# Own products in fp32 instead of split fp16, and 16 of 25 transposed blocks copied by VectorE, in a two-layer graph kernel

## The chip, the cores and the metric

The kernel runs on one core of a Trainium2 chip. The metric is the device time of one execution in microseconds (us). Engines are named as in the profile: PE is TensorE's matmul row and PEld its weight loads, DVE is VectorE, ACT is ScalarE, POOL is GpSimd, SP is the engine that issues the DMAs.

## The reference

There are 3125 nodes with 256 features and 50000 edges (`src`, `dst`, sorted by `dst`). What is computed, cut to its core:

```
# block 0: twice, with (W0, b0), (W1, b1)
deg   = number of edges of each row;  vals = 1 / max(deg, 1)[rows]
neigh = segment_sum(vals * x[cols], rows)
x     = relu(concat(x, neigh) @ W.T + b)
x     = layernorm(x_in + x)
# block 1
h_self = x @ W_self;  h_sparse = keep the 32 largest of each row of (x @ W_neigh)
x      = layernorm(x + h_self + segment_sum(h_sparse[src], dst) / max(deg_dst, 1))
```

## The kernel before

The kernel turns the list of edges into a dense matrix of counts, C, of 3125 x 3125 in fp16, and every sum over neighbours into matmuls with blocks of C. Nodes are cut into 25 blocks of 125.

**Head.** The edges are loaded and turned into a table of slots of up to 128 edges. Matmuls with one-hot `pick` matrices (line 1363, twice: a first set of 125 columns, a second of 500; 100 rows deep) fetch the slots. PE's clock is kept up by matmuls on a tile of ones, 128 rows deep (`keep_clock`, line 1327). The weights W0 and W1 are transposed on PE (`weights_t`) and copied out (`weights_out`, line 1030) to `w_t[0]` and `w_t[1]`. The semaphore `matched` then selects the fast branch (`quick_copies`, `fills`); a slow branch for other lists of edges is not run here.

**Build.** For t = 0 to 24 one slab of C, 125 rows by 3125 columns, is made in four sets of windows (7, 6, 6 and 6). For each set, DVE writes one-hot matrices (`quick_hots`, line 639), PE multiplies them (`fill`, line 1380) into one of two PSUM pairs, and ACT copies the result out (`quick_copy`, line 1078). SP stores the slab to DRAM (line 351). One step later the slab is also transposed, block by block, on PE (`transposes`, line 1459) in four groups g; groups 0 and 2 are copied to `ct` by ACT (`tr_copy`, line 1116), groups 1 and 3 by DVE (line 782). `TG` gives the blocks in each group: 5, 8, 5, 7. DVE writes the one-hots of step t+1 during step t. Each engine works in the order in which `fills`, `quick_copies` and DVE's loop have the calls; the rest is done by semaphores.

**Own products.** For each block t of x the kernel needs x @ [W0 self half | W0 neighbour half]. PE transposes the block into PSUM bank 7 (`own_transposes`, line 1479, fp32). ACT scales it and writes it in fp16 (`own_t`, line 1121), and DVE writes the fp16 rest (`own_low`, line 775). PE then does six fp16 matmuls of 512 columns with the split weights `w0_parts` (`own_product`, line 1467, three for each half h). ACT copies the result from bank 6 to `own` (`own_copy`, line 1128). SP stores one half of `own` (line 355); POOL splits the other into two fp16 parts for the first aggregation (`split_a0`, lines 520 and 522). The table `OWN` says in which step each product stands: none before step 4, one in most steps, two in steps 7, 9, 11 and 13.

**Scales.** The fp16 splits need a scale for each tensor. ACT sums squares of x, of the two weights of block 1 and of the bias (`square_x`, `square_weights`), takes roots (`roots`), PE transposes the statistics and broadcasts the scales (`bounds_t`, `bounds_row`, `scales_b`), and DVE computes them (`bound_rows`, `bounds`, `scales_out`; lines 727 to 764) in steps 2 and 3. The weights are split by `w_high` (ACT, line 1138) and `w_low` (DVE, line 770), six of each. The split weights of the later products are stored to DRAM after slab 6 (line 364); ACT waits for them at the start of step 8 (`w_stored`), since the tiles are then written over.

**After the build** come two aggregations of 1250 matmuls in all (line 1567) with products between them, and the last sum with 625 (line 1679). The change does not touch them.

Of the kernel before, what the change touches and what calls it, by code (L numbers as in the profile page):

```python
# [70 lines left out]
TG = [5, 8, 5, 7]  # L71
TG0 = [0, 5, 13, 18]
# [9 lines left out]
def gnn(nc, x, src, dst, w0, b0, w1, b1, wself, wneigh, out):  # L82
    ctx = ExitStack()
    with ctx:
# [52 lines left out]
        w0_parts = bld("w0_parts", [128, 2, 2, 2 * F], F16)  # L137
        x_t16 = bld("x_t16", [128, 4, 128], F16)
        w_junk = x_t16[:, :, :].rearrange("p k n -> p (k n)")
# [10 lines left out]
        w_t = [held[l]("w_t%d" % l, [128, 4, F], F32) for l in range(2)]  # L150
# [7 lines left out]
        squares = held[5]("squares", [128, 10], F32)  # L158
        norms = held[5]("norms", [128, 10], F32)
# [117 lines left out]
        squared, rooted = sem("squared"), sem("rooted")  # L277
# [9 lines left out]
        own_tlo, own_staged, a0_hi, a0_split = sem("own_tlo"), sem("own_staged"), sem("a0_hi"), sem("a0_split")  # L287
# [21 lines left out]
        def halves(i):  # L309

            if i < 4:
                l, h = divmod(i, 2)
                out = (w0_parts, w_parts[0])[l][:, h].rearrange("p q (a f) -> p q a f", a=2)
                return out[:, 0], out[:, 1], w_t[l][:, h::2, :], scales[:, 3 + l:4 + l]
            at = (i - 4) * F
            out = w_parts[1][:, :, :, at:at + F]
            return out[:, :, 0, :], out[:, :, 1, :], (ws_nat, wn_nat)[i - 4][:, :, :], scales[:, 1 + i:2 + i]
# [9 lines left out]
        def _(sp):  # L327
# [134 lines left out]
        def _(pool):  # L462
# [20 lines left out]
            nc.gpsimd.memset(squares[:, :], 0.0).then_inc(const_ready, 1)  # L483
# [80 lines left out]
        NCONST = 24  # L564
# [3 lines left out]
        def _(dve):  # L568
# [155 lines left out]

            def bound_rows():
# [4 lines left out]
            def bounds():  # L730
# [9 lines left out]

                step(v.tensor_tensor(bound[:, :], sv[:, 0, 0::2], sv[:, 0, 1::2], ALU.max))
# [4 lines left out]
                step(v.tensor_scalar(bound[:, 2:3], sparse_sum[:, :], 1.43 * F ** 0.5, None, ALU.mult))  # L746
# [81 lines left out]
            with dve.If(total > E - 1):  # L828
                for t in range(1, NT):
                    more, own = t + 1 < NT, OWN[t]  # L830
                    if more:
                        quick_hots(t + 1, 0)
                    if t == 3:
# [9 lines left out]
                    if 2 < t < 6:  # L843
                        w_low(2 * t - 5)
                    if t == 3:
                        own_low(0)
# [4 lines left out]
                    if t == 2:  # L851
                        bounds()
# [3 lines left out]
                    if len(own) > 1:  # L856
                        own_low(own[1] + 1)
# [4 lines left out]
            with dve.If(total < E):  # L862
                general_table()
                clear_tr()
                bound_rows()
# [4 lines left out]
                for i in range(6):  # L870
                    w_low(i)
                with dve.Fori(1, NT) as t:
                    for u in range(WT):
# [3 lines left out]
                        if u == 2:  # L877
                            own_low(t - 1)
                own_low(NT - 1)
# [125 lines left out]
        def _(act):  # L1005
# [41 lines left out]
            def square_x(c):  # L1047
                act.wait_ge(x_loaded[c], BOTH)
                if c:
# [3 lines left out]
                             accum_out=squares[0:P, c:c + 1]).then_inc(squared, 1)  # L1053

            def square_weights():
                act.wait_ge(eye_added, 2)
                act.wait_ge(wn_loaded, 16)
                act.wait_ge(b_loaded, 16)
                for k, (m, n) in enumerate(((ws_nat[:, :, :].rearrange("p c f -> p (c f)"), 2 * F),
                                            (wn_nat[:, :, :].rearrange("p c f -> p (c f)"), 2 * F), (bcol[:, :], 2))):  # L1060
                    act.wait_ge(squared, 4 + k)
                    a.activation(w_junk[:, 0:n], m, ACT.Square, scale=TINY, accum_out=squares[:, 4 + 2 * k:5 + 2 * k]).then_inc(squared, 1)

            def roots():
                act.wait_ge(squared, 7)
                a.activation(norms[:, :], squares[:, :], ACT.Sqrt).then_inc(rooted, 1)
                act.wait_ge(rooted, 1)
                a.activation(stat[:, 0:4], norms[:, 0:4], ACT.Copy, scale=1.0 / TINY).then_inc(stat_ready, 1)
# [663 lines left out]
```

## Time and profile before

| what | value |
|---|---|
| three timed runs | 697.01, 697.11, 700.86 us; median 697.11 us |
| the profiled execution | 701.42 us, span 699.6 us |
| busy in the span | PE 641.8 (92%), DVE 505.9 (72%), ACT 348.7 (50%), POOL 106.9 (15%) |
| build loop, steps 1 to 24 | from 36 to 194 us of the span |
| DMA | 73.08 MB, mean 104 GB/s |

Times in a row are us from the start of the span. Starts are recorded more sharply than ends: neighbours on one engine overlap in the records, so what an instruction takes of its engine is read from its start to the next start. PEclk is the granted clock of TensorE as a share of 2.4 GHz.

### The profile page before, as it was taken

To read this page: it belongs to the slowest core of one execution; us is meant where nothing else is said; L and a number is where in the kernel's file an instruction comes from. 1 tells how busy PE (TensorE), PEld (TensorE's weight loads), DVE (VectorE), ACT (ScalarE), POOL (GpSimd) and SP (SyncE) were. 2 spreads that over 40 slices of the span, in tenths; PEclk is the share of its full clock that TensorE was granted. 3 is DMA by queue.
4 is the path that set the end of the run, shared out by engine and by line. 5 is a ranking of instruction groups with operands and counts; after the bars stand their busy time and mean duration, and the time that the engine had idled before them with its cause. 6 is when DMAs were issued, how large, how long until landed. Compare 5 with 4: busy or idle time off the path is not lost.

```text
span 699.6 us, 11372 instructions
## 1 busy us (share of the span) xinstructions
PE 641.8 (92%) x4012; PEld 338.4 (48%) x4013; DVE 505.9 (72%) x1296; ACT 348.7 (50%) x669; POOL 106.9 (15%) x188
## 2 busy tenths in 40 slices
PE   8867788888787999999999999999999889999996
PEld 3355566666643444444444444444444334444443
DVE  8659989999768788888883578787877844634433
ACT  3588888899847777777774223333333220100000
POOL 3001222222111001010100222323232210000000
PEclk9789999999998999999999999999999999999999
DMA  9423554555531011111111555555656414310000
GB/s 212 91 91 113 188 162 137 162 161 158 157 101 37 29 43 33 41 34 40 36 40 39 156 174 164 172 167 169 176 162 182 121 36 135 115 47 23 22 28 25
DMA packets 39542, 73.08 MB, mean 104 GB/s; under 512 B 3120, under 2 KB 32207, under 8 KB 39481
## 3 DMA queue, kind: packets, MB, share of 16 engines
q1 hardware_dynamic: 39481, 72.30, 34.8%
q8 instruction: 34, 0.56, 0.4%
q14 instruction: 27, 0.22, 0.1%
HBM read 38.91 MB, written 33.38 MB: 103 GB/s over the span
## 4 chain that ended last, share of the span: by engine, by line
PE 72%; DVE 17%; ACT 7%; issue 2%; DMA 2%; POOL 0%; SPq 0%; ACTq 0%; DVEq 0%; POOLq 0%
PE pair L1567 36%; PE bank L1679 9%; PE pair L1679 8%; PE bank L1467 7%; DVE hots L639 6%; PE pair L1467 4%; PE bank L1459 2%; DVE ct L782 2%; ACT own L1128 2%; DVE x_t L775 2%; PE bank L1473 1%; PE pair L1363 1%; DMA own_in<-own_dram 1%; ACT x_t L1121 1%; ACT slab L1078 1%
## 5 line engine op out<-in xcount | busy, mean ns | idle before, releaser
L1567 PE MATMUL pair<-xs,ct 125*128 125x512 f16 x625 | 144.1, 381 | 0.0
L1567 PE MATMUL pair<-a,ct 125*128 125x512 f16 x625 | 142.8, 379 | 0.0
L639 DVE TENSOR_TENSOR hots<-iota,jobs 125x1792 f16<-125x1792 f16 (+1 forms) x100 | 104.5, 1063 | 1.3 <-PE pair L1380 0.7
L1567 PEld LDWEIGHTS pair<-xs,ct 125*128 125x128 f16 x625 | 61.3, 100 | 68.7 <-issue 1.8
L1567 PEld LDWEIGHTS pair<-a,ct 125*128 125x128 f16 x625 | 61.0, 99 | 68.1
L1078 ACT ACTIVATE slab<-pair 125x875 f16<-125x875 f32 (+1 forms) x100 | 83.4, 858 | 5.6 <-PE pair L1380 4.1
L1245 ACT ACTIVATE a<-ct 125x1000 f16<-125x1000 f16 (+1 forms) x75 | 80.2, 1069 | 0.9
L1679 PE MATMUL bank<-xs,ct 125*128 125x512 f16 (+1 forms) x325 | 71.5, 379 | 0.0
L1679 PE MATMUL pair<-xs,ct 125*128 125x512 f16 x300 | 66.4, 379 | 0.0
L1459 PE MATMUL bank<-ident,slab 125*128 125x125 f16 x625 | 52.7, 224 | 14.0 <-DVE ct L782 9.9
L1318 ACT ACTIVATE sd<-mv,epsb 125x1 f32<-125x1 f32 x25 | 7.4, 294 | 113.9 <-DVE mv L998 113.9
L531 POOL TENSOR_TENSOR own_in<-own_in,bias_sb 125x256 f32<-125x256 f32 x50 | 37.2, 744 | 173.8 <-DMA own_in<-own_dram 173.7
L1380 PE MATMUL pair<-hots 125*128 125x125 f16 x625 | 52.8, 224 | 11.5 <-ACT slab L1078 8.4
L895 DVE SCALAR_TENSOR_TENSOR t<-pair,rdeg,own_in 125x256 f32<-125x256 f32 x50 | 24.2, 484 | 54.2 <-PE pair L1567 48.3
L1459 PEld LDWEIGHTS bank<-ident,slab 125*128 125x128 f16 x625 | 40.2, 101 | 27.1 <-issue 14.4
L1221 ACT ACTIVATE tr_sb<-bank 128x500 f16<-128x500 f32 x50 | 29.0, 580 | 45.1 <-PE bank L1473 45.1
L1679 PEld LDWEIGHTS bank<-xs,ct 125*128 125x128 f16 (+1 forms) x325 | 32.3, 100 | 37.8
L1380 PEld LDWEIGHTS pair<-hots 125*128 125x128 f16 x625 | 41.1, 100 | 17.0 <-issue 11.7
L1467 PE MATMUL bank<-w_parts,x_t 128*125 128x512 f16 x150 | 41.2, 383 | 7.5 <-DVE x_t L775 7.5
L1679 PEld LDWEIGHTS pair<-xs,ct 125*128 125x128 f16 x300 | 29.8, 99 | 34.4
L782 DVE COPY ct<-bank 125x1008 f16<-125x1008 f16 (+1 forms) x50 | 32.0, 641 | 15.3 <-PE bank L1459 15.3
L1467 PE MATMUL pair<-w_lay,tr_sb 128*128 128x512 f16 x150 | 36.9, 382 | 3.8 <-ACT tr_sb L1221 3.8
(213 smaller groups left out, 852.9 us busy)
## 6 DMA issues: line engine op xcount, KB each, us to landing
c_dram<-slab SPq DMA_DIRECT2D x25, 683.6 KB
ct<-c_dram SPq DMA_DIRECT2D x25, 683.6 KB
own_in<-own_dram SPq DMA_DIRECT2D x50, 125.0 KB
own_dram<-own SPq DMA_DIRECT2D x25, 125.0 KB
own_dram<-own_st SPq DMA_DIRECT2D x25, 125.0 KB
x_in<-in_x_dram SPq DMA_DIRECT2D x25, 125.0 KB
z_dram<-z_st SPq DMA_DIRECT2D x25, 125.0 KB
a<-z_dram SPq DMA_DIRECT2D x5, 625.0 KB
```

Of the source, the lines that this page charges most:

```text
L531: nc.gpsimd.tensor_tensor(own_in[k % 2][:, :], own_in[k % 2][:, :], bias_sb[:, :], ALU.add).then_inc(own_biased, 1)
L639: v.tensor_tensor(hots[k][:, :, :, :].rearrange("p w g (a d) -> p (w g) a d", d=2), iota, job, ALU.is_equal).then_inc(win_hot, 1)
L782: v.tensor_copy(ct[:, TG0[g]:TG0[g] + TG[g], t, :], tr16[1][0:P, 0:TG[g], 0:PC]).then_inc(tr_free[1], 1)
L895: return noted(v.scalar_tensor_tensor(t2[k % 2][:, :], agg[k % 3][0:P, 0:F], rdeg[l][:, T:T + 1], own_in[k % 2][:, :], ALU.mult, ALU.add))
L1078: a.activation(slab3[t % 2][:, :, lo * QW:hi * QW].rearrange("p b (w d) -> p b w d", d=QW), pair[f % 2][0:P, 0:n, 0:QKEY].rearrange("p w ( ...
L1221: a.activation(tr_sb[i % 2][:, :, 0:P], tp[i % 2], ACT.Copy).then_inc(tp_copied, 1)
L1245: a.activation(unread[:, 0:(hi - lo) * P].rearrange("p (b s) -> p b s", s=P), ct[:, lo:hi, T, 0:P], ACT.Copy, accum_out=deg_part[:, T, k:k ...
L1380: last = mm(pair[f % 2][:, u, 0:QKEY], hots[f][:, u, 0, :], hots[f][:, u, 1, 1:QKEY + 1], start=True, stop=True, skip_group_check=True)
L1459: last = nc.tensor.transpose(tr16[g % 2][:, i, 0:P], slab[par][:, (TG0[g] + i) * P:(TG0[g] + i) * P + 128], ident16[:, 0:P])
L1467: last = mm(out, lhs(2 * pt + h), w[:, h, q, :], start=h == 0 and k == 0, stop=h == 1 and k == 2, skip_group_check=True)
L1567: ins = mm(agg[k % 3][0:lhs.shape[1], :], lhs, parts[l][:, t, :], start=t == 0, stop=t == NT - 1, skip_group_check=True)
L1679: ins = mm(out3[T % 8][0:lhs.shape[1], :], lhs, xs[:, b, :], start=b == 0, stop=b == NT - 1, skip_group_check=True)
```

## The change

Four things are changed.

1. The own products are done in fp32. `own_t` writes the transposed block unscaled in fp32, `own_low` is gone, each half of a product is one fp32 matmul call with 512 columns, and the W0 split (two of six `w_high` and `w_low`) is gone. `own_copy` uses another scale. The tile of W0 moves out of the place that is reused later.
2. `TG` becomes 4, 8, 5, 8: ACT copies 9 blocks in a step where it copied 10, DVE 16 where it copied 15.
3. Products start at step 3 and two stand in steps 8, 13 and 18 alone. The scales come earlier: `bounds_t`, `bounds_row` and `scales_b` are all in step 2. The statistics of the last part of x, of the weights of block 1 and of the bias are now largest absolute values found by DVE in step 1, where ACT had summed squares; the square root is done by DVE as one more small instruction on the bits.
4. In the head, one `keep_clock` matmul of 512 columns follows each group of three pick matmuls of the second set (eight in all), behind a wait for `wt_copied`. The `keep_clock` matmuls of step 2 are gone.

```diff
-OWN = {0: [], 1: [], 2: [], 3: [], 4: [0], 5: [1], 6: [2], 7: [3, 4], 8: [5], 9: [6, 7], 10: [8], 11: [9, 10], 12: [11],
-       13: [12, 13], **{t: [t] for t in range(14, NT)}}
+TWOS = (8, 13, 18)
+OWN = {t: [] for t in range(3)}
+for _t in range(3, NT):
+    _n = sum(map(len, OWN.values()))
+    OWN[_t] = [_n, _n + 1] if _t in TWOS else [_n]
-KEEP = {0: 4, 1: 2, 2: 1}
+KEEP = {0: 4, 1: 2}
-TG = [5, 8, 5, 7]
+TG = [4, 8, 5, 8]
...
+            def largest_x(c):
+                dve.wait_ge(x_loaded[c], BOTH)
+                v.tensor_reduce(stat[0:P, c:c + 1], xs32[:, XC[c]:XC[c + 1], :].rearrange("p t f -> p (t f)"), X, ALU.max,
+                                apply_absolute_value=True).then_inc(stat_ready, 1)
...
-            def own_low(t):
-
-                dve.wait_ge(own_tcopied, t + 1)
-                v.scalar_tensor_tensor(x_t16[:, 2:4, 0:P], xp, scales[:, 0:1], x_t16[:, 0:2, 0:P], ALU.mult, ALU.subtract
-                                       ).then_inc(own_tlo, 1)
...  (DVE's loop)
+                    if t == 1:
+                        largest_x(3)
+                    if t == 2:
                         dve.wait_ge(cols_copied, 4)
-                        scales_out()
+                        bound_rows()
                     tr_copy(t - 1, 1)
-                    if 2 < t < 6:
+                    if 2 < t < 5:
                         w_low(2 * t - 6)
...
+                    if t == 1:
+                        largest_w()
                     if t == 2:
-                        bound_rows()
+                        bounds()
...
-                    if own and own[0] + 1 < NT:
-                        own_low(own[0] + 1)
...
+                    if t == 2:
+                        scales_out()
...  (ACT)
-                a.activation(x_t16[:, 0:2, 0:P], xp, ACT.Copy, scale=scales[:, 0:1]).then_inc(own_tcopied, 1)
+                a.activation(x_t32[:, :, :], xp, ACT.Copy).then_inc(own_tcopied, 1)
...
-                    if t == 1:
-                        square_x(3)
-                    if t == 1:
-                        square_weights()
-                    if t == 1:
-                        roots()
...  (PE)
+                        if k:
+                            keep_clock(bank[7], 1)
                 last.then_inc(picked, 1)
+                if k == 0:
+                    pe.wait_ge(wt_copied, 2)
...
-                    pe.wait_ge(own_tlo, t + 1)
+                    pe.wait_ge(own_tcopied, t + 1)
                     pe.wait_ge(own_copied, t + 1)
-                    pe.wait_ge(w_split, 2)
-                last = in_parts(bank[6][0:P, :], lambda k: x_t16[:, k, 0:P], w0_parts, (h,))
+                    pe.wait_ge(wt_copied, 2)
+                last = mm(bank[6][0:P, :].rearrange("p (a f) -> p a f", a=2), x_t32[:, h, :], w0_t[:, h::2, :], start=h == 0, stop=h == 1,
+                          skip_group_check=True)
...  (SP)
-                    sp.wait_ge(w_split, 6)
+                    sp.wait_ge(w_split, 4)
```

In PE's loop, the second half of a product now stands ahead of the transposes of group 1, where it stood behind them.

## Rows read from the trace of the kernel before

**Rows 1.** The page, part 4: the chain that ended last, shares by engine.

```profile
PE 72%; DVE 17%; ACT 7%; issue 2%; DMA 2%; POOL 0%; SPq 0%; ACTq 0%; DVEq 0%; POOLq 0%
```

**Rows 2.** Busy time by stretch: length, PE, PEld, DVE, ACT, POOL, clock, DMA.

```profile
157.00:168.00 11.00, 9.20 (x114) 7.09 (x112) 10.88 (x15) 9.89 (x16) 2.39 (x4) 1.00 0.52 165
...
16.00:26.00 10.00, 10.00 (x24) 3.21 (x25) 6.59 (x15) 2.89 (x5) 0.00 (x0) 0.51 0.98 190
```

**Rows 3.** Timeline of one late step, DVE, then POOL: start, us, instruction.

```profile
171.08 0.67 DVE L782 COPY ct<-bank 125x1008 f16<-125x1008 f16 x1
171.67 0.94 DVE L639 TENSOR_TENSOR hots<-iota,jobs 125x1536 f16<-125x1536 f16 x1
172.67 0.48 DVE L775 SCALAR_TENSOR_TENSOR x_t<-bank,scales,x_t 128x250 f16<-128x250 f32 x1
173.07 2.23 DVE L639 TENSOR_TENSOR hots<-iota,jobs 125x1536 f16<-125x1536 f16 x2
175.22 0.60 DVE L782 COPY ct<-bank 125x882 f16<-125x882 f16 x1
175.75 1.07 DVE L639 TENSOR_TENSOR hots<-iota,jobs 125x1792 f16<-125x1792 f16 x1
...
172.95 0.67 POOL L522 TENSOR_TENSOR xs<-own,xs 125x256 f16<-125x256 f32 x1
```

**Rows 4.** Timeline of ACT: the same place in two late steps.

```profile
171.59 0.69 ACT L1128 ACTIVATE own<-bank,unscale 125x512 f32<-125x512 f32 x1 [0.56 <-PE bank L1467]
...
177.26 0.69 ACT L1128 ACTIVATE own<-bank,unscale 125x512 f32<-125x512 f32 x1 [0.55 <-PE bank L1467]
```

**Rows 5.** Timeline of PE in that step.

```profile
171.39 0.38 PE L1479 MATMUL bank<-identx,xs 125*128 125x125 f32 x2
171.61 0.50 PE L1380 MATMUL pair<-hots 125*128 125x125 f16 x6
...
176.41 0.81 PE L1467 MATMUL bank<-w_parts,x_t 128*125 128x512 f16 x3
177.06 0.38 PE L1479 MATMUL bank<-identx,xs 125*128 125x125 f32 x2
```

**Rows 6.** Timeline of DVE: first one-hots issued in steps 5, 9, 11 and 23.

```profile
70.45 1.08 DVE L639 TENSOR_TENSOR hots<-iota,jobs 125x1792 f16<-125x1792 f16 x1
...
96.09 1.08 DVE L639 TENSOR_TENSOR hots<-iota,jobs 125x1792 f16<-125x1792 f16 x1
...
109.41 1.08 DVE L639 TENSOR_TENSOR hots<-iota,jobs 125x1792 f16<-125x1792 f16 x1
...
181.42 1.08 DVE L639 TENSOR_TENSOR hots<-iota,jobs 125x1792 f16<-125x1792 f16 x1
```

**Rows 7.** Instructions of line 1394, two fp32 matmul calls: count, min/median/max ns.

```profile
L1394 PE MATMUL bank<-onesq,hits x4: 163/163/164, 32.7 to 32.8; 125*1 125x1 f32 x4
```

**Rows 8.** Timeline of DVE in steps 1 to 3; last, line 651's group.

```profile
36.66 1.09 DVE L639 TENSOR_TENSOR hots<-iota,jobs 125x1792 f16<-125x1792 f16 x1 [0.32 <-PE pair L1380]
...
49.71 0.68 DVE L782 COPY ct<-bank 125x1008 f16<-125x1008 f16 x1 [4.21 <-PE bank L1459]
...
52.44 0.17 DVE L739 COPY sv<-bank 1x32 f32<-1x32 f32 x1
...
54.74 0.16 DVE L752 TENSOR_SCALAR srow<-svi 1x8 f32<-1x8 f32 x1
...
58.94 0.75 DVE L770 SCALAR_TENSOR_TENSOR w_parts<-w_t,scales,w_parts 128x512 f16<-128x512 f32 x1 [0.43 <-ACT w_parts L1138]
...
L651 DVE TENSOR_REDUCE stat<-w_nat 128x1 f32<-128x512 f32 x4 | 2.5, 674 | 0.0
```

**Rows 9.** Timeline of ACT and SP around the store of the split weights.

```profile
80.81 1.64 ACT L1078 ACTIVATE slab<-pair 125x750 f16<-125x750 f32 x2
...
82.46 1.89 SPq L364 DMA_DIRECT2D wparts_dram<-w_parts  x2
...
89.24 0.93 ACT L1078 ACTIVATE slab<-pair 125x875 f16<-125x875 f32 x1 [0.35 <-DMA wparts_dram<-w_parts]
```

More of the change, by code:

```diff
@@ L149, in gnn @@
         held = [Arena(ct_at + (b * REG + HELD * PC) * 2, ct_at + (b + 1) * REG * 2) for b in range(19, NT)]
-        w_t = [held[l]("w_t%d" % l, [128, 4, F], F32) for l in range(2)]
+        w_t = [w0_t, held[1]("w_t1", [128, 4, F], F32)]
         ws_nat = held[2]("ws_nat", [128, 2, F], F32)
@@ L745, in bounds @@
                 step(v.tensor_tensor(sparse_sum[:, :], sv[:, 1, 12:13], sv[:, 1, 13:14], ALU.add))
-                step(v.tensor_scalar(bound[:, 2:3], sparse_sum[:, :], 1.43 * F ** 0.5, None, ALU.mult))
+                step(v.tensor_scalar(bound[:, 2:3], sparse_sum[:, :], 1.01 * F ** 0.5, None, ALU.mult))
                 step(v.tensor_scalar(bound[:, 5:6], bound[:, 5:6], 1.0, None, ALU.add))
@@ L864, in _ @@
                 clear_tr()
+                largest_x(3)
+                largest_w()
                 bound_rows()
@@ L869, in _ @@
                     general_hots(u)
-                for i in range(6):
+                for i in range(4):
                     w_low(i)
@@ L1052, in square_x @@
                 a.activation(x_junk[:, 0:n], xs32[:, XC[c]:XC[c + 1], :].rearrange("p t f -> p (t f)"), ACT.Square, scale=TINY,
[L1053 to L1068, printed above, removed]
-                a.activation(stat[:, 10:16], norms[:, 4:10], ACT.Copy, scale=1.0 / TINY).then_inc(stat_ready, 1)
+                             accum_out=stat[0:P, c:c + 1]).then_inc(squared, 1)
             def quick_copy(t, f):
@@ L1127, in own_copy @@
                 act.wait_ge(a0_split, t + 1)
-                a.activation(own[:, par, :], bank[6][0:P, :], ACT.Copy, scale=unscale[0:P, 4:5]).then_inc(own_copied, 1)
+                a.activation(own[:, par, :], bank[6][0:P, :], ACT.Copy, scale=scales[0:P, 1:2]).then_inc(own_copied, 1)
             def ready_for_own():
@@ L1170, in quick_copies @@
                         own_copy(own[1], own[1] % 2, own[1] // 2)
-                        own_t(own[1] + 1)
-                    if 2 < t < 5:
-                        w_high(2 * t - 4)
-                        w_high(2 * t - 3)
+                        if own[1] + 1 < NT:
+                            own_t(own[1] + 1)
                 for g in (0, 2):
@@ L1181, in copies @@
                 ready_for_own()
-                for i in range(6):
+                for i in range(4):
                     w_high(i)
@@ L1206, in _ @@
                 square_x(2)
-                square_x(3)
-                square_weights()
-                roots()
                 act.wait_ge(win_read, FILLS - 1)
@@ L1416, in bounds_t @@
             def bounds_t():
-                pe.wait_ge(stat_ready, 2)
+                pe.wait_ge(squared, 3)
+                pe.wait_ge(stat_ready, 4)
                 pe.wait_ge(w_sums, 4)
@@ L1526, in fills @@
                     transposes(t - 1, par, 0)
+                    fill(t, 1)
                     if t == 2:
-                        bounds_t()
-                    fill(t, 1)
+                        bounds_row()
                     if t in KEEP:
                         keep_clock(bank[7], KEEP[t])
-                    transposes(t - 1, par, 1)
                     if own:
                         own_product(own[0], 1)
-                    if t == 3:
+                    transposes(t - 1, par, 1)
+                    if t == 2:
                         own_transposes(0, xs32[:, 0, :])
@@ L1543, in fills @@
                     if t == 2:
-                        bounds_row()
+                        scales_b()
                     if len(own) > 1:
@@ L1551, in fills @@
                         own_product(own[1], 1)
-                        own_transposes(own[1] + 1, xs32[:, own[1] + 1, :])
+                        if own[1] + 1 < NT:
+                            own_transposes(own[1] + 1, xs32[:, own[1] + 1, :])
                     transposes(t - 1, par, 3)
```

69 lines of the change are left out of this document (34 added, 35 removed).

## The prediction

> **What bounds the kernel now.** I read the page's chain first: PE holds 72% of it and DVE 17% [rows 1]. The aggregations and the last sum are PE alone, and the change leaves them as they are; DVE's share lies in the build. So only the stretch up to 194 us can move, and what follows it moves along by the same amount. The busy times by stretch come next. In a late stretch of 11 us DVE is busy 10.88, PE 9.20, ACT 9.89, at full clock (1.00, which is 2.4 GHz), with the DMA engines at 0.52 [rows 2]. DVE is full, the DMA is not. The timeline of one step says the same without the overlap of records: ACT's `own` copies stand 5.67 us apart and ACT has an idle gap of 0.55 before each [rows 4], while DVE goes from one instruction to the next without a gap: 0.59 for the 8-block copy, 1.00 for a set of one-hots (its last 0.1 is a wait for ACT's `own_t`, whose end `own_low` needs), 0.40 for `own_low`, 2.15 for two sets, 0.53 for the 7-block copy, 1.00 for the wide set. That is 5.67 [rows 3]. A step with one product is bound by DVE.
>
> In the steps before 14, singles and doubles alternate. From step 9 to step 11, three products, DVE's first one-hots move on by 13.32 [rows 6], 1.98 more than two singles. There the chain product, `own_copy`, `own_t`, `own_low`, next product is the bound, and the same kind of group takes every step pair from 7 to 13.
>
> **The change, part by part.** The sum is made on the profiled execution, 701.42 us, which lies 4.3 above the median of 697.11; I carry the difference over to the median, since nothing in the build's steady rows depends on which run it is.
>
> *DVE in a single step.* Removed: `own_low`, 0.40, and the wait of 0.13 before it (1.00 against 0.87 for a set that has no wait, the rate of the second set of the pair). Added: one block on the last copy, 0.59 for 0.53, so 0.06. 5.67 - 0.53 + 0.06 = 5.20; I use 5.21. In it is a stall: the pair of sets takes 2.15 where twice 0.87 would be 1.74, and POOL's subtraction runs from 172.95 while the first of them starts at 173.07 [rows 3]. After the change `own_copy` starts about when PE comes to group 1's transposes, so POOL's cast and subtraction end up beside the set behind the 8-block copy, again with the subtraction a little ahead of it. I keep 0.41.
>
> *PE in a single step.* Three fp16 matmuls of 512 columns take 0.65 from their first start, 176.41, to that of the next instruction, 177.06, so one is 0.216 [rows 5]. The rows of before show no fp32 matmul of that width. Two rows bound it. A call in fp32 leaves two records: line 1394 has two calls and four records [rows 7]. A record in fp32 with 125 columns (line 1479) takes 0.11, from 171.39 to 171.61 for two, and one in fp16 with as many 0.055, from 171.61 for six [rows 5]. Lower bound: two records at the fp16 rate, 0.43 for a half. Nearest row: two records at twice the rate, 4 x 0.216 = 0.86. Upper bound: the 0.11 is a fixed cost in part and hides a steeper rate, 4 times per record, 1.72. I take 0.86, since the fp32 row is the one of the same kind. PE then has 50 fills and transposes at 0.055 (2.75), two halves (1.72) and the fp32 transposes (0.22): 4.7, below DVE's 5.21.
>
> *ACT in a single step.* 5.67 - 0.55 = 5.12 occupied, less one block of about 0.1: 5.0. The fp32 output of `own_t` is taken at the price of the fp16 one. ACT too is below 5.21, but by 0.2 alone. Laid out in order (fill 0.34 to 0.39, half 0.86, group 0, fill, half, group 1, own transposes, fill, group 2, fill, group 3), PE reaches group 1 about 0.5 before DVE has freed its bank, so DVE stays the bound. Behind the product's second half, which moved ahead of group 1's transposes, waits DVE's copy of that group; those 0.5 cover it, and without them a single would be 5.7.
>
> *Double steps.* From group 1: own transposes, fill, group 2, 1.3; the second product waits for `own_t`, until 1.5; its halves, the fill between and the own transposes, 2.3; group 3, 0.4; then the next step's first fill and the wait for ACT's second `own_t`, until 4.9; half, group 0, fill, half, 2.3. Sum 7.2, and the step behind it gains 0.1: 7.1. ACT waits in it, not DVE.
>
> *Steps 5 to 22.* Before, 70.45 to 181.42, 111.0 [rows 6]. After, 15 x 5.21 + 3 x 7.1 = 99.5. **-11.5.**
>
> *Steps 1 to 4.* Before, 36.66 to 70.45, 33.8, in which DVE was idle 4.21 before one copy alone, waiting for PE and, through it, for the squares and roots of ACT [rows 6, 8]. After, DVE has 16 sets (14.4), 8 copies (4.7), `largest_x` of 1536 columns at the 0.60 that 512 take from start to start (0.674 recorded; 1.8), `largest_w` (1.3), `bound_rows` (0.4), `bounds` with 13 small instructions (2.3 for 12 from 52.44 to 54.74, so 2.5), `scales_out` (0.6), four `w_low` of 0.75 recorded, 0.65 taken (2.6) [rows 8], two stalls by POOL (0.8), and 1.5 of waits for PE's group 1 in steps 1 and 2, the second behind `bounds_row`, for which PE now stops until `bound_rows` is done. Sum 30.6 to 31.0. **-2.8.** ACT loses 5 us of squares, roots and a table load here; it is not the bound, and I count nothing more for that.
>
> *Store of the split weights.* SP issues it 1.65 after ACT's fourth copy of step 6 starts (80.81 to 82.46), and ACT is released at 89.24, 6.8 after the issue [rows 9]. Before, a double step lay between and the wait was 0.35. Now only 5.21 + 0.7 - 1.65 = 4.3 lie between the issue and the first copy of step 8, so ACT will stand for 2.5, and step 8 is a double, where ACT is on the path. **+2.0** (0 to 2.5).
>
> *Head.* Eight matmuls of 512 columns are added to 24 picks that lie on the chain. From 16 to 26 us PE is busy for all of 10.00 us, and the clock stays at 0.51, its lower level of 1.2 GHz [rows 2]. At that level the eight cost 8 x 0.43 = 3.4 and give nothing. If they bring the clock to the upper level at once, the picks take 5 where they took 10 and the eight cost 1.7, so -3.3. If the clock rises part of the way through, about -1. I take **-1**. The Trainium skill ("TensorE: Matmul & The Clock Gate", section "What's actually happening") says that the gate's ratio follows how busy PE has been. By that rule these picks would have run at full speed and the eight would be +1.7; rows 2 speak against it as stated, since PE was busy throughout and the clock stayed low. The wait for `wt_copied` costs nothing: the copies are ahead of ACT's first `slots_out`, which is done by then.
>
> *Tail and rest.* In step 23 DVE's saving and in step 24 the longer product (0.43) cancel: 0. DMA: about 0.9 MB of slab and own rows each step, 0.52 of the engines at 5.67, 0.57 at 5.21: covered.
>
> Sum: -11.5 - 2.8 + 2.0 - 1.0 = -13.3, so 688.1 for the profiled execution and **683.8** for the median.
>
> **The rivals.**
>
> *A, the stall by POOL changes.* If POOL's pair falls clear of the one-hots, DVE needs 4.8 and ACT's 5.0 is the bound, with its order 4.9 to 5.0: 18 steps x 0.25 = 4.5 less, 679. If both POOL instructions stop DVE (the cast is 0.53 recorded, 0.4 alone), 0.4 x 18 = 7 more, 691. For the second speaks that DVE now has one-hots back to back where `own_low` stood. The Trainium skill ("SBUF — State Buffer", section "Who interferes with whom") says that a DVE instruction with two inputs in SBUF and a GpSimd one that reads it exclude each other, first come first served. The stall of 0.41 in rows 3 agrees; the rule lets either order come out.
>
> *B, the head stays at the low clock.* +3.4 in place of -1: 688. For it: ten microseconds at full use did not raise the clock. Against it: the tile of ones is dense and fills the array, and the picks are one-hot and 100 rows deep.
>
> *C, PE becomes the bound, slower than before.* If a half takes more than 1.2, PE's own work passes DVE's: 4.7 + 2 x (1.2 - 0.86) = 5.4, with the order's gaps 5.7. That is the point. At the upper bound of 1.72 PE needs 6.4 in a single and about 10 in a double: 15 x 6.4 + 3 x 10 = 126 against 111, +15; with the rest 697 + 15 - 3 + 1 = 710. Only the small fp32 rows speak on it, and they speak for 0.86.
>
> *D, a product ahead of group 1 delays it.* The move of the second half costs DVE a wait in each step, singles stay at 5.6 to 5.7, and only doubles, three for four, and the early steps pay: 691 to 693. Against it: the 0.5 of room in the layout.
>
> **How the numbers follow.** Forecast as summed (679 to 688, singles at 5.0 to 5.4): 0.60. A's gain 0.08, A's loss 0.08, B 0.13 (which still is 688), D 0.06, C 0.05. A measurement of this kernel can tell about 1%, 7 us, from no change. Faster by more than that, under 690.1: the forecast, A's gain, B and a part of A's loss: 0.87. Within 1%: the rest of A's loss and D: 0.09. Slower: 0.04. The range leaves out C and half of D and of A's loss above, and little below: 677 to 691.
>
> **What would show it.** Right: own products of 0.86 a half, no line 775, singles of 5.2 with DVE without gaps, doubles of about 7.1, an ACT gap of 2 to 3 by the store of the split weights at step 8, and a clock above 0.51 in the stretch of the second picks. Wrong: halves over 1.2, gaps of DVE before the copy of group 1 in every step, or second picks that take longer than before.

## The result and the profile after

| | median us | runs | ratio to before (95%) |
|---|---|---|---|
| before | 697.14 | 697.01, 697.11, 697.18, 700.86 | |
| after | 689.93 | 688.79, 689.49, 690.37, 690.46 | 0.9892 [0.9864, 0.9921] |
| after, on a second chip | 691.04 | six, 689.56 to 694.91 | 0.9894 [0.9855, 0.9932] |

The kernel became 7.2 us faster, 1.1%. The forecast was 683.8, 13.3 faster, with a range of 677 to 691: the sign and the range held, the size was about half. The steady steps did what was forecast; steps 1 to 4, where 2.8 were to be won, lost time.

The page of the kernel after: span, busy times, the granted clock in 40 slices, the chain that ended last.

```profile
span 688.5 us, 11240 instructions
...
PE 649.0 (94%) x3966; PEld 335.5 (49%) x3967; DVE 498.1 (72%) x1274; ACT 338.6 (49%) x654; POOL 106.4 (15%) x187
...
PEclk9967999999999999999999999999999899999999
...
PE 84%; DVE 8%; ACT 3%; DMA 2%; issue 2%; SPq 0%; POOL 0%; DVEq 0%; ACTq 0%; POOLq 0%
```

DVE's share of the chain fell from 17% [rows 1] to 8% and PE's rose from 72% to 84%. The third and fourth slices of the clock (34 to 69 us) have 6 and 7: that is the early part of the build.

**A steady step.** DVE in one step (start, us, instruction):

```profile
136.47 0.67 DVE L791 COPY ct<-bank 125x1008 f16<-125x1008 f16 x1
137.07 3.04 DVE L637 TENSOR_TENSOR hots<-iota,jobs 125x1536 f16<-125x1536 f16 x3
140.03 0.67 DVE L791 COPY ct<-bank 125x1008 f16<-125x1008 f16 x1
140.63 1.07 DVE L637 TENSOR_TENSOR hots<-iota,jobs 125x1792 f16<-125x1792 f16 x1
141.62 0.67 DVE L791 COPY ct<-bank 125x1008 f16<-125x1008 f16 x1
```

Against [rows 3], `own_low` is gone, both copies have eight blocks, and there is no gap. The step takes 141.62 - 136.47 = 5.15, where it took 5.67. The three sets take 2.96; three at 0.87 would be 2.61, so 0.35 is a stall. It lies beside POOL's subtraction:

```profile
136.89 0.67 POOL L520 TENSOR_TENSOR xs<-own,xs 125x256 f16<-125x256 f32 x1
```

PE in the step:

```profile
137.31 0.60 PE L1445 MATMUL bank<-ident,slab 125*128 125x125 f16 x8
...
138.24 1.08 PE L1479 MATMUL bank<-w_t,x_t 128*125 128x512 f32 x2
139.16 0.39 PE L1445 MATMUL bank<-ident,slab 125*128 125x125 f16 x4
139.38 0.50 PE L1365 MATMUL pair<-hots 125*128 125x125 f16 x6
139.71 1.08 PE L1479 MATMUL bank<-w_t,x_t 128*125 128x512 f32 x2
```

One half of a product is two records and holds PE for 0.92, from 138.24 to 139.16. Three fp16 matmuls of the same width took 0.65 [rows 5].

**Stretches by engine** (window, length, PE, PEld, DVE, ACT, POOL, clock, DMA share, GB/s): the head, the early steps, and a late stretch as in [rows 2].

```profile
16.00:26.00 10.00, 10.00 (x58) 4.70 (x56) 7.95 (x17) 5.24 (x8) 0.00 (x0) 1.00 1.06 189
46.00:59.00 13.00, 9.11 (x50) 6.23 (x50) 6.98 (x25) 4.83 (x7) 0.40 (x1) 0.50 0.19 61
...
137.00:148.00 11.00, 10.82 (x117) 7.57 (x115) 11.00 (x14) 10.63 (x18) 2.70 (x5) 1.00 0.54 170
```

In the late stretch DVE is full and ACT and PE are close to it. In the second row nothing is full: DVE works 6.98 of 13.00, PE 9.11, and the clock stands at 0.50, 1.2 GHz.

**Step 3.** DVE in it, then PE (in brackets the idle time before an instruction, and its releaser):

```profile
52.61 0.15 DVE L780 TENSOR_TENSOR unscale<-unscale,scales 128x1 f32<-128x1 f32 x1
52.68 1.08 DVE L637 TENSOR_TENSOR hots<-iota,jobs 125x1792 f16<-125x1792 f16 x1
58.68 0.68 DVE L791 COPY ct<-bank 125x1008 f16<-125x1008 f16 x1 [4.92 <-PE bank L1445]
...
65.01 1.08 DVE L637 TENSOR_TENSOR hots<-iota,jobs 125x1792 f16<-125x1792 f16 x1
```

```profile
52.91 2.04 PE L1479 MATMUL bank<-w_t,x_t 128*125 128x512 f32 x2 [0.78 <-issue]
54.74 0.62 PE L1445 MATMUL bank<-ident,slab 125*128 125x125 f16 x4
...
55.79 2.02 PE L1479 MATMUL bank<-w_t,x_t 128*125 128x512 f32 x2
57.60 1.04 PE L1445 MATMUL bank<-ident,slab 125*128 125x125 f16 x8
```

DVE finishes the scales (`scales_out`, last row at 52.61), and 0.3 later PE starts the first product, after an idle time of 0.78. The fp32 product does not read the scales. But it waits for `own_copied`, which ACT first raises in `ready_for_own`, once DVE has written the last scale (`unscale_ready`); and it writes bank 6, where the scales stand until DVE has copied them, at 52.05. The halves take 1.83 and 1.81, and the eight transposes of group 1, for which DVE waits, start at 57.60. So DVE stands for 4.92, and step 3 takes 65.01 - 52.68 = 12.33, where step 3 of the kernel before took 7.57 and 7.56 in two profiled executions.

**The store of the split weights.** SP issues it, and ACT waits for it at the start of step 8. SP, then ACT:

```profile
81.50 1.90 SPq L363 DMA_DIRECT2D wparts_dram<-w_parts  x2
```

```profile
88.69 0.92 ACT L1068 ACTIVATE slab<-pair 125x875 f16<-125x875 f32 x1 [2.81 <-DMA wparts_dram<-w_parts]
```

DVE's first one-hots of steps 8, 9 and 10, which answer to [rows 6]:

```profile
87.52 1.07 DVE L637 TENSOR_TENSOR hots<-iota,jobs 125x1792 f16<-125x1792 f16 x1
95.34 1.59 DVE L637 TENSOR_TENSOR hots<-iota,jobs 125x1792 f16<-125x1792 f16 x1
102.44 1.07 DVE L637 TENSOR_TENSOR hots<-iota,jobs 125x1792 f16<-125x1792 f16 x1
```

A double step shows in these marks one step later, since DVE is ahead: 7.10 in step 9 is the double of step 8, and the 7.82 in step 8 hold ACT's wait.

**Where the time went**, by the same marks in each profiled execution: DVE's first one-hots of steps 0, 1, 5 and 23, as in [rows 6], then the first matmul of the first aggregation and the start of its last one. Before was profiled twice; the second execution (696.29 us) lies nearer to the median.

| us | before, first | before, second | after | after - first | after - second |
|---|---|---|---|---|---|
| until the one-hots of step 0 | 32.60 | 28.42 | 29.63 | -3.0 | +1.2 |
| step 0 | 4.06 | 4.44 | 4.40 | +0.3 | 0.0 |
| steps 1 to 4 | 33.79 | 32.14 | 37.98 | +4.2 | +5.8 |
| steps 5 to 22 | 110.97 | 111.0 | 101.66 | -9.3 | -9.3 |
| tail of the build | 12.0 | 12.2 | 10.6 | -1.4 | -1.6 |
| first aggregation | 183.4 | 182.1 | 180.2 | -3.2 | -1.9 |
| all behind it | 322.8 | 324.2 | 324.0 | +1.3 | -0.2 |

### The profile page after: what moved, and what is told of

Read it like the earlier page. It is cut to its first block, busy times and chain, and to the rows that moved or that the text cites. A ratio compares the mean times of both kernels' runs of the same rounds, so it can differ in the third digit from the quotient of the medians.

```text
span 688.5 us, 11240 instructions
## 1 busy us (share of the span) xinstructions
PE 649.0 (94%) x3966; PEld 335.5 (49%) x3967; DVE 498.1 (72%) x1274; ACT 338.6 (49%) x654; POOL 106.4 (15%) x187
## 4 chain that ended last, share of the span: by engine, by line
PE 84%; DVE 8%; ACT 3%; DMA 2%; issue 2%; SPq 0%; POOL 0%; DVEq 0%; ACTq 0%; POOLq 0%
PE pair L1555 36%; PE bank L1667 10%; PE pair L1667 9%; PE bank L1479 6%; PE bank L1445 5%; PE pair L1453 5%; PE bank L1453 5%; PE pair L1365 4%; DVE hots L637 2%; PE bank L1459 1%; DMA own_in<-own_dram 1%; DMA wparts_dram<-w_parts 1%; PE pair L1344 1%; PE bank L1465 1%; ACT a L1226 1%
## 5 line engine op out<-in xcount | busy, mean ns | idle before, releaser
L1068 ACT ACTIVATE slab<-pair 125x875 f16<-125x875 f32 (+1 forms) x100 | 83.2, 856 | 11.4 <-PE pair L1365 7.0
L1479 PE MATMUL bank<-w_t,x_t 128*125 128x512 f32 x100 | 56.0, 642 | 1.8 <-ACT x_t L1111 1.0
L1365 PEld LDWEIGHTS pair<-hots 125*128 125x128 f16 x625 | 41.4, 101 | 10.2 <-issue 7.8
L791 DVE COPY ct<-bank 125x1008 f16<-125x1008 f16 x50 | 33.7, 673 | 14.5 <-PE bank L1445 14.5
```

Of the source, the lines that this page charges most:

```text
L791: v.tensor_copy(ct[:, TG0[g]:TG0[g] + TG[g], t, :], tr16[1][0:P, 0:TG[g], 0:PC]).then_inc(tr_free[1], 1)
L1068: a.activation(slab3[t % 2][:, :, lo * QW:hi * QW].rearrange("p b (w d) -> p b w d", d=QW), pair[f % 2][0:P, 0:n, 0:QKEY].rearrange("p w ( ...
L1365: last = mm(pair[f % 2][:, u, 0:QKEY], hots[f][:, u, 0, :], hots[f][:, u, 1, 1:QKEY + 1], start=True, stop=True, skip_group_check=True)
L1479: last = mm(bank[6][0:P, :].rearrange("p (a f) -> p a f", a=2), x_t32[:, h, :], w0_t[:, h::2, :], start=h == 0, stop=h == 1, skip_group_ch ...
```

## The experiments

Times of runs are medians; the ratio is to the kernel before, timed in the same set of runs (its medians there: 697.39, 697.53 and 697.04).

### Head: the fillers alone, and the change without them

e3 puts the eight fillers into the kernel before; e4 is that kernel unchanged, for a second profile of it; e2 takes the fillers out of the change.

```diff
(e3, against before)
+                        if k:
+                            keep_clock(bank[7], 1)
                 last.then_inc(picked, 1)
+                if k == 0:
+                    pe.wait_ge(wt_copied, 2)
(e2, against after)
-                        if k:
-                            keep_clock(bank[7], 1)
```

> The kernel before with the eight matmuls among the second picks alone, behind the same wait. Theory 1: 694 (3 us under 697.1), picks ending near 23.6 us with the clock at 1.00. Rival (the low clock in the head of the profiled execution was peculiar to it, which was 4.3 above the median): 697 to 699, since typical executions of before ran their picks at full clock already and the eight only add 1.7.

> The kernel before, unchanged, for a second trace. The profiled execution of before was 701.4 against a median of 697.1. If the low clock during the picks (16 to 26 us, worth 3 us) is peculiar to that execution, this one ends its picks near 22 us; if it is there in every execution, they end near 26.8 again, and a time near 697 lacks something else: the two low stretches at 208 and 219 us, in the first aggregation, which cost some 3 us against the changed kernel's trace.

> The changed kernel without the eight matmuls on the tile of ones among the second picks; all else is as in the changed kernel. Theory 1: they keep the clock up through the picks (1.00 from 16 to 26 us against 0.51 before) and are worth the 3.0 us by which the head ended earlier; then this kernel takes 692.5 to 693.5 and its picks end near 26.8 us at the low clock. Rival: the clock of that stretch falls in some executions only, by the moment at which the program starts; then this kernel's picks may run at full clock as well, end 1.7 us earlier than the changed kernel's, and the time is 688 to 690.

Measured: e3 698.75, 0.9997 [0.9966, 1.0027]; e2 691.50, 0.9930 [0.9902, 0.9958], against 0.9892 and 0.9894 for the change with them. The stretch 16 to 22 us of e4 (no fillers), and then of e5 (below, with fillers), columns as above:

```profile
16.00:22.00 6.00, 6.00 (x31) 2.52 (x29) 5.28 (x15) 2.89 (x5) 0.00 (x0) 1.00 1.13 222
```

```profile
16.00:22.00 6.00, 6.00 (x17) 2.04 (x15) 5.28 (x14) 2.89 (x5) 0.00 (x0) 0.50 1.13 222
```

The second picks run at the upper level without fillers and at the lower one with them; the row of before [rows 2] had them at the lower level too. Of the four profiled executions without fillers, two had a low clock in the picks (before and e12); of the ten with them, six, e8 among them, for which the upper level was expected. At the upper level the one-hots of step 0 come at 27.8 and 28.4 without the fillers and at 29.1 to 29.6 with them; where 6.8 us are at the lower level, at 31.1 and at 32.2 to 32.7. So at an equal clock the fillers cost about 1.2 to 1.3 by the means (29.35 against 28.1, and 32.4 against 31.1), with 0.7 to 1.8 between single executions. Four executions and ten are too few to say whether fillers change how often the clock is low. In the medians 1.3 us, 0.2%, can't be told from nothing.

### Steps 1 to 4: missing fillers, or the product ahead of group 1

There were two theories on step 3. The first: the clock is low because the fillers of step 2 are gone. The second: PE's queue has the first product, which waits until the scales are written, ahead of group 1's transposes, which don't wait for that, and the low clock makes this longer. e1 gives step 2 fillers again, eight where before had four; e5 starts the products at step 4, so that none stands in step 3; e6 does both, with two fillers at each place; e8 is the change unchanged.

```diff
(e1: after each of the first two places of KEEP in fills)
+                    if t == 2:
+                        keep_clock(bank[7], 4)
(e5; in e6 also KEEP = {0: 4, 1: 2, 2: 2})
-TWOS = (8, 13, 18)
-OWN = {t: [] for t in range(3)}
-for _t in range(3, NT):
+TWOS = (8, 12, 16, 20)
+OWN = {t: [] for t in range(4)}
+for _t in range(4, NT):
...  (ACT's own_t(0) and PE's own_transposes(0))
-                    if t == 2:
+                    if t == 3:
```

> The changed kernel with four matmuls on the tile of ones behind the first and behind the second fill of step 2, eight in all (the kernel before had one behind each of the four fills). Step 3 took 12.33 us in the changed kernel's trace, where I had forecast 6.4, with the clock at 0.50 from 46 to 59 us. Theory 1: the clock fell because TensorE has little to do in step 2 and stayed low into step 3, where the fp32 halves take 0.98 per record at that clock against 0.48. Then this kernel's step 3 is 6 to 8 us, the stretch from 46 to 59 is mostly at 1.0, and the time is 684 to 686 (4 to 6 under the changed kernel's 689.9). Rival: the clock falls in that stretch whatever step 2 holds, since it is the fp32 halves and the waits of step 3 that keep it low, or the step is long through the wait for the scales; then step 3 stays at 11 to 13 us and the time at 689 to 691, plus up to 1 for the eight matmuls.

> The changed kernel with its products from step 4 on (transposes of block 0 in step 3, doubles in steps 8, 12, 16 and 20) in place of step 3 (doubles in 8, 13, 18). In the changed kernel VectorE was idle 4.92 us in step 3 ahead of its copy of group 1. Theory 2: TensorE's in-order queue held it up: the first product waits for the scales (VectorE's last work of step 2) and both its fp32 halves stand ahead of group 1. Then step 3 falls from 12.3 to about 7.5, step 4 stays near 7, and the fourth double costs 1.9: 3 us net, 686 to 688 beside 689.9. Rival (theory 1 in its weak form: the clock at its low level alone makes step 3 long): step 3 stays at 9 us or more, since the clock is low there with the product or without, and the time is 689 to 692.

> The kernel of the run before this one (products from step 4) with two matmuls on the tile of ones behind each of the four fills of step 2. Theory 1: they shorten the stretch at the low clock around step 3 and step 3 is a further 1 us shorter. Rival: as with the eight matmuls put into step 2 of the changed kernel, where step 2 grew to 12.1, the low stretch stays and they cost 0 to 2 us.

> The changed kernel, unchanged, beside the others on one chip and with more rounds: 0.989 of the kernel before again (0.986 to 0.992). In its trace, singles of 5.15 to 5.2 and doubles of 7.1 whatever the head does; step 3 between 10.5 and 12.5; the clock of the second picks at its upper level throughout or for most of it.

| | median, ratio (95%) | steps 1, 2, 3, 4 | sum | DVE idle in it |
|---|---|---|---|---|
| before, second | | 7.43, 10.48, 7.56, 6.67 | 32.1 | 6.4 |
| after | 689.93, 0.9892 [0.9864, 0.9921] | 8.64, 10.01, 12.33, 7.00 | 38.0 | 9.5 |
| e8 after again | 691.04, 0.9894 [0.9855, 0.9932] | 8.32, 10.42, 11.49, 7.00 | 37.2 | 8.7 |
| e1 | 692.90, 0.9922 [0.9897, 0.9948] | 8.55, 12.13, 10.77, 7.00 | 38.5 | 10.0 |
| e5 | 690.19, 0.9864 [0.9821, 0.9906] | 8.20, 10.43, 7.42, 7.00 | 33.1 | 4.6 |
| e6 | 690.51, 0.9896 [0.9858, 0.9934] | 8.64, 11.28, 7.73, 7.00 | 34.7 | 6.0 |

DVE in step 3 of e5; compare the copy with that at 58.68 above.

```profile
55.48 1.08 DVE L637 TENSOR_TENSOR hots<-iota,jobs 125x1792 f16<-125x1792 f16 x1
56.73 0.68 DVE L791 COPY ct<-bank 125x1008 f16<-125x1008 f16 x1 [0.17 <-PE bank L1445]
...
62.90 1.08 DVE L637 TENSOR_TENSOR hots<-iota,jobs 125x1792 f16<-125x1792 f16 x1
```

Without a product in step 3, the wait is 0.17 instead of 4.92, though the clock is at its lower level there too, until 56.4; and the step takes 7.42 instead of 10.92 to 12.33 (six profiled executions with the product there and no fillers in step 2). The second theory is shown. Fillers in step 2 are not the cure: with e1's step 2 grows by 1.7 to 2.1, and DVE still waits 3.56 before the copy in step 3; in e6 they cost 1.2 over e5 in steps 2 and 3.

The clock has a large share in it all the same. In e1 the second half of the product ran at the upper level:

```profile
57.26 2.04 PE L1479 MATMUL bank<-w_t,x_t 128*125 128x512 f32 x2 [0.78 <-issue]
...
60.12 1.08 PE L1479 MATMUL bank<-w_t,x_t 128*125 128x512 f32 x2
...
61.68 0.68 DVE L791 COPY ct<-bank 125x1008 f16<-125x1008 f16 x1 [3.56 <-PE bank L1445]
```

The wait is 1.4 shorter there than in after. e2, without any of these fillers, had most of its second half at the upper level too and waited 3.71, so this isn't the fillers' doing. With the first half (0.92 less) and what stands between the halves (0.51 less) at the upper level as well, 2.1 of wait would be left: an estimate from e1's rows, since no run had it so. By that estimate over half of the 4.92 is the low clock, and the rest the place of the product. The lower level lasts 13.6 us around step 3 in after, 10.3 in e5, 10.2 in e6 with its fillers, and 3.4 in before's second execution; why it lasts so long in the kernels of the change stays open. Nor did a run change the order alone: the second half, which the change moved ahead of group 1, is 1.81 of the 4.92; the first half stood ahead of group 1 before as well.

e5 pays for its gain with a fourth double step, 1.9, and the store of the split weights is still in it. By the median it is level with the change (690.19 for 691.04 in the same set of runs; 686 to 688 was expected), by its ratio a little ahead, with intervals that overlap.

### Steps 8 and 9: the store of the split weights

e7 moves the first double step to 7, as a double step lay there before. e9 is e5 with the store issued one slab earlier, which the earlier scales allow.

```diff
(e7)
-TWOS = (8, 13, 18)
+TWOS = (7, 13, 18)
(e9: e5, and on SP)
-                if t == HELD - 2:
+                if t == HELD - 3:
```

> The changed kernel with the first double step at 7 in place of 8. The split weights are stored after slab 6 and ScalarE waits for them at the start of step 8; with the double between, the wait has 2 us more of cover. Forecast: steps 7 to 9 take 7.1 + 5.2 + 5.2 plus a wait of 0 to 0.6, so about 2 us less than the 5.16 + 7.82 + 7.10 of the changed kernel, in the trace and in the time (688). Rival: the 2.6 us in steps 8 and 9 are the double's own and move to step 7 with it: then no change.

> The changed kernel with products from step 4 (doubles in 8, 12, 16, 20) and the split weights stored after slab 5 in place of slab 6, one step earlier than where ScalarE stands for them. This is the version that the runs so far point to. Forecast: steps 1 to 4 take 33.0 (37 to 38 in the changed kernel), steps 8 and 9 take 12.3 together (14.9 to 16.6), steps 5 to 22 101.1 with four doubles; 686.5 to 688, about 0.985 of the kernel before. Rival: the earlier store meets the slab stores and only moves the wait to the slab copies of steps 6 and 7; then steps 5 to 22 stay at 103 to 104 and the time at 690.

Measured: e7 689.16, 0.9856 [0.9820, 0.9891]; e9 **686.49** (685.48 to 688.10), 0.9841 [0.9802, 0.9881]. First one-hots of steps 7 to 10 in e7:

```profile
84.04 1.07 DVE L637 TENSOR_TENSOR hots<-iota,jobs 125x1792 f16<-125x1792 f16 x1
89.21 1.59 DVE L637 TENSOR_TENSOR hots<-iota,jobs 125x1792 f16<-125x1792 f16 x1
96.52 1.07 DVE L637 TENSOR_TENSOR hots<-iota,jobs 125x1792 f16<-125x1792 f16 x1
101.98 1.07 DVE L637 TENSOR_TENSOR hots<-iota,jobs 125x1792 f16<-125x1792 f16 x1
```

and of steps 8, 9 and 10 in e9, and the issue of its store:

```profile
81.95 1.08 DVE L637 TENSOR_TENSOR hots<-iota,jobs 125x1792 f16<-125x1792 f16 x1
87.38 1.58 DVE L637 TENSOR_TENSOR hots<-iota,jobs 125x1792 f16<-125x1792 f16 x1
94.47 1.08 DVE L637 TENSOR_TENSOR hots<-iota,jobs 125x1792 f16<-125x1792 f16 x1
```

```profile
70.78 1.88 SPq L363 DMA_DIRECT2D wparts_dram<-w_parts  x2
```

Steps 7 to 9 take 17.95 in e7 (84.04 to 101.98) and 5.16 + 7.82 + 7.10 = 20.1 in after. Steps 8 and 9 take 12.52 in e9 (81.95 to 94.47) and 14.92 in after (87.52 to 102.44), at the same number of products. So the store cost 2.1 to 2.4 against these two, and 2.6 against a single and a double of the steady kind (5.2 + 7.1). In e8, e1, e2 and e10, four of the eight profiled executions with this wait, step 8 took 9.3 to 10.3, with 3.4 us of it at the lower clock: there the wait came to 4.2 or more over a single. e9 is faster than the kernel before, clear of noise. Against the change its ratio is lower by 0.005, with intervals that overlap at their ends: likely faster, not shown.

### The steady step: POOL, the block, and own_low alone

e10 takes away POOL's read beside the one-hots (a memset in place of the subtraction, so the low part of the first aggregation's operand is left out). e11 gives the block back to ACT. e12 is the kernel before with `own_low` left out (so that part of the own products is not computed), all else as it was.

```diff
(e10)
-                nc.gpsimd.tensor_tensor(xs[:, t, F:2 * F], a0, xs[:, t, 0:F], ALU.subtract).then_inc(a0_split, 1)
+                nc.gpsimd.memset(xs[:, t, F:2 * F], 0.0).then_inc(a0_split, 1)
(e11)
-TG = [4, 8, 5, 8]
+TG = [5, 8, 5, 7]
(e12, against before: DVE, then PE)
-                dve.wait_ge(own_tcopied, t + 1)
-                v.scalar_tensor_tensor(x_t16[:, 2:4, 0:P], xp, scales[:, 0:1], x_t16[:, 0:2, 0:P], ALU.mult, ALU.subtract
-                                       ).then_inc(own_tlo, 1)
+                pass
-                    pe.wait_ge(own_tlo, t + 1)
+                    pe.wait_ge(own_tcopied, t + 1)
```

> The changed kernel in which GpSimd writes zeros where it subtracted (the low fp16 part of the own product is left out), so it reads nothing from SBUF in that instruction. In the changed kernel's single step one set of one-hots takes 1.23 from start to start beside the subtraction, and 0.87 without. If the subtraction alone causes that, VectorE needs 4.83, ScalarE's 5.0 becomes the bound, and singles are 4.9 to 5.0; 15 singles and 3 doubles give 3 to 4 us, 686 to 687. Rival: ScalarE or TensorE already set 5.19 and VectorE's stall is cover: singles stay at 5.15 to 5.2.

> The changed kernel with the transposed blocks shared as before: 5, 8, 5 and 7, so VectorE copies 15 and ScalarE 10. If VectorE is the bound of a single step, singles fall by 0.06 to 5.12, about 1 us in all, below what the timing can tell. If ScalarE is close behind, its extra block of 0.1 takes that back and singles are 5.1 to 5.2; if it was ScalarE that bound, they are 5.3 and the time is 1 to 2 us more.

> The kernel before, six fp16 matmuls for each product and all, with VectorE's fp16 rest of the transposed block left out (the matmuls read what the tile holds, so that part of the product is wrong). It shows what taking 0.53 from VectorE is worth without the fp32 products. Forecast: singles 5.14 (5.67 before), two steps with three products 12.2 (13.3 before), steps 1 to 4 as before at 32 to 34, so steps 5 to 22 100 to 102 against 111.0, and the time 687 to 688. Rival: in fp16 the doubles are bound by the chain through ScalarE and stay at 7.5; then steps 5 to 22 take 104 to 105.

Measured: e10 691.22, 0.9891 [0.9838, 0.9944]; e11 689.83, 0.9902 [0.9870, 0.9934]; e12 691.18, 0.9899 [0.9848, 0.9951]. DVE in one step of e10, of e11 and of e12, and POOL in that of e12:

```profile
138.04 0.68 DVE L791 COPY ct<-bank 125x1008 f16<-125x1008 f16 x1
138.64 2.69 DVE L637 TENSOR_TENSOR hots<-iota,jobs 125x1536 f16<-125x1536 f16 x3
141.25 0.67 DVE L791 COPY ct<-bank 125x1008 f16<-125x1008 f16 x1
141.84 1.08 DVE L637 TENSOR_TENSOR hots<-iota,jobs 125x1792 f16<-125x1792 f16 x1
142.97 0.68 DVE L791 COPY ct<-bank 125x1008 f16<-125x1008 f16 x1
```

```profile
141.68 3.15 DVE L637 TENSOR_TENSOR hots<-iota,jobs 125x1536 f16<-125x1536 f16 x3
144.75 0.60 DVE L791 COPY ct<-bank 125x882 f16<-125x882 f16 x1
```

```profile
150.52 0.67 DVE L780 COPY ct<-bank 125x1008 f16<-125x1008 f16 x1
151.11 3.35 DVE L639 TENSOR_TENSOR hots<-iota,jobs 125x1536 f16<-125x1536 f16 x3
154.39 0.61 DVE L780 COPY ct<-bank 125x882 f16<-125x882 f16 x1
...
155.91 0.67 DVE L780 COPY ct<-bank 125x1008 f16<-125x1008 f16 x1
```

```profile
151.78 0.53 POOL L520 CAST xs<-own 125x256 f16<-125x256 f32 x1 [3.53 <-ACT own L1126]
152.39 1.26 POOL L522 TENSOR_TENSOR xs<-own,xs 125x256 f16<-125x256 f32 x1
```

*POOL.* Three sets take, from start to start, 2.61 in e10 (138.64 to 141.25), 2.96 in after, 3.07 in e11, 3.28 in e12. So the subtraction costs DVE 0.35 in after. In e12 POOL's pair costs 0.67: the cast falls beside the first and second set, the subtraction beside the second and third, and it is itself held up (1.26 for 0.67). The Trainium skill ("SBUF — State Buffer", section "Who interferes with whom") says that a DVE instruction with two inputs in SBUF and a GpSimd one that reads it shut each other out. These runs agree, in 0.35 and 0.67 a step. In e10 a step takes 4.93: from 138.04 to 142.97; DVE has a gap of 0.14 (141.84 to 142.97 for one-hots that take 0.99 in after) and ACT none, so ACT is the bound, near the 5.0 of the forecast. Steps 5 to 22 take 100.5, for 103.2 to 103.4 in e1, e2 and e8, which like it have the clock at the lower level in step 8. Its median (691.22, where 686 to 687 was expected) doesn't show these 2.8 us: four runs leave an interval of 0.5% on either side.

*The block.* Singles take 5.19 to 5.20 in e11, but for a first one of 5.09, and 5.15 to 5.21 in after. The block moved 0.07 to DVE's copy, and the stall beside the sets is 0.11 smaller (2.96 for 3.07). The two cancel; the sixteenth block is worth nothing that can be measured.

*own_low alone.* In e12 singles take 5.40 (forecast 5.14, missed by the second stall), step pairs with a double 12.0 (12.6 from step 9 to 11), where before had 13.32 [rows 6], and steps 5 to 22 103.2, outside the 100 to 102 that were expected. So of the 111.0 before, 7.7 go with `own_low` alone, with no change in number format or order; the change as made takes 9.3, or 11.4 with the first double at step 7 (e7: 99.6). And e12 keeps steps 1 to 4 at 32.4, 5.6 under after, while after is ahead by 1.6 in steps 5 to 22 and by 1.2 in the tail. By these e12 would be 2.8 ahead. The medians (691.18 for 689.93) don't show it; in e12's profiled execution the picks and the first aggregation, at a lower clock than in after's, took 4.2 back. So the two can't be told apart here, and `own_low` alone gives most of the gain.

## Why the prediction was right, and where not

**Right: the single step.** 5.21 forecast, 5.15 to 5.21 measured. Each term holds: no `own_low`, no wait for `own_t`, a stall of 0.35 for 0.41. A half took 0.91 (0.92 above) for 0.86: the nearest row, the small fp32 one [rows 5], at twice the fp16 rate for each of two records, was the right one of three bounds. Rival C is refuted by it, and D by the timeline, where DVE has no gap before group 1's copy. Rival A's mechanism exists, as e10 and e12 show at both of its ends; in this order neither end came.

**Right: doubles and the store.** Doubles 7.10 for 7.1. ACT waited 2.81 for the store where 2.5 were forecast, at a cost of 2.1 to 2.6 for 2.0. Steps 5 to 22 were to take 99.5 + 2.0 = 101.5, and took 101.66: singles a little shorter and the store a little dearer nearly cancel.

**Wrong: steps 1 to 4, the step of the prediction that failed.** 31.0 forecast, 36.6 to 38.5 measured in the seven profiled executions that have a product in step 3. The sum there was one of DVE's own work with 1.5 us of waits, and DVE's idle time was 9.5. Put 8.0 more of waits into the sum: 39.0, against 38.0. In e9 the same sum with its 4.5 of idle time gives 34.0, against 33.0. So the work was priced 1 us too high in both, and the waits are the miss. The prediction said that behind the product's second half waits DVE's copy of group 1, and that 0.5 us of room covers it. It drew that from a steady step. In step 3 the first product waits for the scales, DVE's last work of step 2, so there is no room; and the prediction priced a half at 2.4 GHz, while the clock there was at 1.2, where a half takes 1.83. Rival D, which was this mechanism, was priced in every step or in none, and not in the first step alone. Against the second execution of before, step 3 is 4.8 of the 5.8 lost; step 1, where DVE has `largest_x` and `largest_w`, is 1.2.

**Wrong: the head.** -1 forecast; where the clock is the same, +1.2 to +1.3. That the executions differ in the clock at the same code was not seen, as only one was profiled: the one shown lay 4.3 above the median in part because its picks ran at the lower level. "I carry the difference over to the median" holds for the steady steps, not for the head. Rival B named the mechanism, for this kernel and not for single executions.

**Not forecast: the tail, -1.4 to -1.6 for 0.** 0.5 of it is step 23, a single step that the sum had set against the longer product. In step 24 the second half of the product stands ahead of group 1, and ACT's `own_copy` comes 5.3 after the one-hots of step 23, where it came 7.2 after. e12, in the old order, has a tail of 11.9. That fits the order as the cause of the rest, but no run changed the order alone. The first aggregation, 180.2 for 182.1 and 183.4, goes with the stretches of low clock in it: 179.9 to 180.9 with none (after, e2, e11), 181.2 to 182.0 with one of 3.4 us (e1, e5, e6, e7, e8, e10), 182.1 to 183.4 with 6.4 to 6.8 us in all. The last group is all four executions with the code of before or close to it (before, e4, e3, e12), and one of the ten others (e9). So the change may be worth 1.5 here (182.9 against 181.4, the means of the four and the ten) by fewer such stretches; what would cause that stays open.

**The sum.** Against the second profile of before, the nearer one to the median: +1.2 + 5.8 - 9.3 - 1.6 - 1.9 - 0.2 = -6.0, where the medians differ by -7.2. The forecast had -1.0 - 2.8 - 9.5 = -13.3. Of the 7.3 between them the early steps are 8.6, the head 2.2, the steady steps 0.2; tail, first aggregation and rest give back 3.7. That 689.93 lies in the range owes something to luck: the upper end of 691 left room for rival D and A's loss, not for the wait in step 3 alone, and the repeat gave 691.04.

## What to carry to other kernels

An in-order queue has no slack in its first rounds: before a new item is put ahead of an old one, ask in the first step that has it what the item waits for and who stands behind it, and not only in the steady state. Here products that start one step later (e5) are worth 3.5 to 4.9 us in the early steps, less 1.9 for the double step that they need, and a store that is issued one slab earlier (e9) 2.4. Take the nearest row of the same kind as the price of an operation that the trace lacks, but read at which clock it will run. And profile the kernel before more than once ahead of a claim on a stretch whose clock varies.

## What the runs showed of the hardware

- An fp32 matmul of 512 columns is two records, 0.91 us together at 2.4 GHz and 1.83 at 1.2 GHz; an fp16 one takes 0.216 at 2.4.
- PE, busy for all of 6.00 us, stood at the clock 1.00 in one execution (e4) and at 0.50 in another (e5), in the same stretch of a head that differs by eight matmuls, and both levels come with and without them.
- With the square roots gone from step 1, the table load in front of the degree sums (line 1245, 1.28 us at 201.3) is gone too: four loads on ACT before, two after. It lay on ACT while PE was in the first aggregation; what it was worth was not measured by itself.
- A DVE stall beside POOL depends on where POOL's pair falls: 0, 0.35, 0.46 and 0.67 us for three sets of one-hots in e10 (a memset in place of the subtraction), after, e11 and e12.
